# Attention on one Trainium2 core: the products with v of two key tiles at a time behind every second step

## What is computed

```python
q = h @ wq / sqrt(d); k = h @ wk; v = h @ wv        # 16 heads of 32
q, k = rotary_pos_emb(q), rotary_pos_emb(k)
logits = einsum('bhik,bhjk->bhij', q, k)
a = softmax(logits, axis=-1)
y = einsum('bhij,bhjv->bhiv', a, v)
```

## Time and profile before

| what | value |
|---|---|
| median of three runs | 3582.47 us (3579.41 to 3586.3) |
| the profiled execution's own time | 3573.79 us |
| its span | 3572.0 us |
| granted TensorE clock over the span | 0.979 of full speed |
| attention in the span | about 387 to 2061 us |
| TensorE (PE) busy | 3420.8 us, 96% |
| VectorE (DVE) busy | 2079.4 us, 58% |
| ScalarE (ACT) busy | 1508.5 us, 42% |
| GpSimd (POOL) busy | 2016.5 us, 56% |

### The profile page before, as it was taken

The page is one execution under the profiler, slowest core; times in us unless marked ns, Lnnn a source line. Parts: engine busy times, 40 slices in busy tenths (PEclk is TensorE's granted clock), DMA queues, the critical chain, the costliest instruction groups (busy, mean ns, idle before and its releaser), DMA issues. The chain is left out here.

```text
span 3572.0 us, 47047 instructions
## 1 busy us (share of the span) xinstructions
PE 3420.8 (96%) x16632; PEld 2230.6 (62%) x16632; DVE 2079.4 (58%) x3331; ACT 1508.5 (42%) x2785; POOL 2016.5 (56%) x1613
## 2 busy tenths in 40 slices
PE   6999899999999999999999959999999995999998
PEld 5777455454554555545455348888888883778877
DVE  6776677777777777777777344222222213454554
ACT  2332466666666666666666632111111112222221
POOL 3644488887978888797888812222222223343342
PEclk9999999999999999999999979999999997999999
DMA  5556677869678686867865543122222114222221
GB/s 193 177 169 205 118 154 138 148 129 154 140 131 152 127 156 133 151 142 132 156 127 107 113 140 107 55 73 75 73 67 75 54 36 139 83 86 76 73 87 41
DMA packets 176737, 419.32 MB, mean 117 GB/s; under 512 B 15382, under 2 KB 62998, under 8 KB 151670
## 3 DMA queue, kind: packets, MB, share of 16 engines
q1 hardware_dynamic: 153606, 249.59, 26.4%
q0 software_dynamic: 22896, 166.73, 24.0%
HBM read 162.25 MB, written 87.03 MB: 70 GB/s over the span
## 5 line engine op out<-in xcount | busy, mean ns | idle before, releaser
L868 DVE TENSOR_REDUCE part_max<-ps_att 128x1 f32<-128x512 f32 x1972 | 1225.4, 683 | 372.2 <-PE ps_att L786 372.1
L914 ACT ACTIVATE probs<-ps_att 128x512 f32<-128x512 f32 x2048 | 1061.7, 603 | 521.9 <-PE ps_att L758 458.7
L965 POOL TENSOR_TENSOR prob_sums<-prob_sums,probs 128x512 f32<-128x512 f32 x884 | 1142.8, 1537 | 60.8 <-DMA probs<-probs 60.8
L810 PE MATMUL ps_att<-probs,v_tok 128*32 128x512 f32 x4096 | 548.3, 607 | 3.1 <-DMA v_tok<-v 3.1
L1456 POOL TENSOR_TENSOR ff_g_lo<-ff_g,ff_g_hi 128x512 fp32r<-128x512 f32 x128 | 164.7, 1287 | 551.5 <-DVE ff_g_hi L1417 551.5
L758 PE MATMUL ps_att<-q_stack,k_stack 97*128 97x512 f32 x768 | 319.8, 424 | 9.9 <-ACT probs L914 9.7
L758 PE MATMUL ps_att<-q_stack,k_first 97*128 97x512 f32 x768 | 324.7, 423 | 2.6 <-ACT probs L914 2.6
L1325 ACT ACTIVATE ff_g<-ps_ff 128x512 f32<-128x512 f32 x128 | 76.5, 597 | 582.2 <-PE ps_ff L1209 582.2
L786 PE MATMUL ps_att<-k_stack,q_stack 96*128 96x512 f32 x768 | 303.8, 396 | 0.0
L786 PE MATMUL ps_att<-k_first,q_stack 96*128 96x512 f32 x756 | 301.9, 399 | 0.0
L1946 POOL TENSOR_TENSOR av_gated_lo<-av_full,av_gated_hi 128x512 fp32r<-128x512 f32 x64 | 94.4, 1475 | 313.9 <-ACT av_gated_hi L1783 313.9
(11 more groups left out here) (209 smaller groups left out, 5514.9 us busy)
## 6 DMA issues: line engine op xcount, KB each, us to landing
probs<-probs POOLq DMA_DIRECT2D x159, 1024.0 KB, 8.6
q_stack<-qk SPq DMA_DIRECT2D x144, 128.0 KB, 6.9
qk<-rot_hi SPq DMA_DIRECT2D x64, 256.0 KB, 7.0
qk<-rot_lo SPq DMA_DIRECT2D x64, 256.0 KB, 5.0
av_gate_rows<-gate SPq DMA_DIRECT2D x64, 256.0 KB
k_stack<-qk SPq DMA_DIRECT2D x24, 512.0 KB, 10.4
k_first<-qk SPq DMA_DIRECT2D x18, 512.0 KB, 10.1
x_in_sb<-in_x SPq DMA_DIRECT2D x8, 1024.0 KB, 6.7
```

The source lines that it names most:

```text
L810: mm = nc.tensor.matmul(o_ps[rows, :], t["v"][:, steps[w]["b"], k, rows], t["p"][:, w % PR, h, :], start=(k == 0), stop=(k == LT - 1))
L868: nc.vector.tensor_reduce(t["pm"][:, r, k:k + 1], mx[mx_uses % 3], AX.X, ALU.max)\
L914: nc.scalar.activation(t["p"][:, at % PR, h, :], sT[(at * G + h) % 3], ACT.Exp)\
L965: nc.gpsimd.tensor_tensor(x, first, t["p"][:, w % PR, h, :], ALU.add).then_inc(s["acc_done"], 1)
```

## The change

In the loop over the steps on TensorE the products with v are no longer made in each step for the step before. They are made at every second step (even `at`), for the two steps before, behind that step's scores and maxima. The sums of TensorE move with them. The two products whose place in the loop depends on other conditions, `last_sums` (at step 5 of a block) and `turn_maxima` (at step 13), stay where they are. At the end of the loop the last two tiles are done in one go. No other engine's instructions change, and their number and operands stay the same.

```diff
@@ -839,20 +839,21 @@
                     score(st, at, i)
                     if st["job"]:
                         maxima(st, i)
-                if at:
-                    values(at - 1)
-                    if by_pe(at - 1):
-                        sums(at - 1)
-                    if at >= LT and at % LT == LAST_AT:
-                        last_sums(at // LT - 1)
+                for w in (at - 2, at - 1) if at and at % 2 == 0 else ():
+                    values(w)
+                    if by_pe(w):
+                        sums(w)
+                if at >= LT and at % LT == LAST_AT:
+                    last_sums(at // LT - 1)
                 if ending is not None:
                     turn_maxima(ending)
                     ending = None
...
-            values(end - 1)
-            sums(end - 1)
+            for w in (end - 2, end - 1):
+                values(w)
+                sums(w)
             last_sums(blocks - 1)
```

## The result

| | before | changed |
|---|---|---|
| median | 3581.69 us (5 runs) | 3604.6 us (5 runs) |
| ratio | | 1.0069, 95% interval 1.0056 to 1.0083 |
| profiled execution, own time | 3573.79 us | 3602.55 us |
| its span | 3572.0 us | 3600.7 us |

A forecast was written before the change was run, and what follows sets the result against it. TensorE's own instruction list was taken to bound the kernel; terms of 11 + 15 + 0 + 1 - 3 + 8 = +32 us on 3582.5 gave 3614 us, with an 8-in-10 range of 3586 to 3640.

The forecast's parts named there:

- What TensorE alone would save: Ordinary pair of attention steps: 5.83 instead of 6.14 us by TensorE's own times, a saving of 0.31 per pair.
- Term A: Ordinary pairs: maxima loads wait for VectorE's reductions on three banks, pair 6.20 instead of 6.14; +11 us (-9 to +22).
- The rule on loads pulled ahead: Maxima weight loads: if pulled ahead even past a semaphore, a pair would be at 6.09 and Term A at -9.
- Term B: Pair with the turn, steps 13 and 14: turn and copy inside the run, pair 6.62, +0.48 each; +15 us (+2 to +22).
- Term C: Pair of steps 5 and 6: last_sums leaves the run four and four as before; 0.
- Term D: Last 19 steps, without maxima: scores wait for exponentials, pair 5.52 against 5.38; +1 us (0 to +2).
- Term E: Start: step 2's scores run while the first v product waits 3.06 us for v's load; -3 us (0 to -6).
- Term F: GpSimd's chain starts 2.3 us later; some 1.3 reaches ScalarE in seven units that load; +8 us (0 to +16).
- Rival 1: Ordinary pairs: maxima waits do not bind and the saving arrives, 3521 us, or 3570 with half; chance 0.08 together.
- Rival 4: Last stretch: TensorE's clock drops through short idles; 25 steps taking twice 3.07 add 77 us, 3691 us; chance 0.02.

The follow-up runs named there:

- The two combined versions without spread loads: Changed kernel with maxima ahead of scores, turn in step 12, last sums at step 6: 3569.07 us; also with tile 0's v product in step 1: 3565.0 us.
- The combined version with spread loads: Changed kernel with maxima first, turn in step 12, last sums at step 6, tile 0's v product in step 1, loads spread over 54 steps: 3555.66 us.

## Why the prediction was right

The sum said +32 us with a range of +4 to +58; it is +23 between the medians. The mechanism that carried 26 of the 32, VectorE's pace against three banks, is the one found, and the two runs with shorter reductions and the run with the turn moved show it. The terms for the start, the end and GpSimd came out otherwise one by one. That their sum fits, +6 forecast (D, E and F) and 3 + 1.6 + 2 in the split of the profiles above, is luck.

- **What TensorE alone would save** (0.31 a pair): right. With the reductions out of the way a pair took 5.79 against 5.83.
- **Term A** (+11): right in mechanism and size. 6.19 for 6.20, the loads released 0.06 after the reduction. Against 6.14 it is 0.05 a pair, 9 us.
- **The rule on loads pulled ahead**, from the Trainium skill, "TensorE: Matmul & The Clock Gate", in its part on what happens when a matmul is issued: in the rows shown no load passed its semaphore; the load unit (PEld) stood idle 0.28 to 0.30 ahead of each of the last three maxima loads of a run. A load that waits is not pulled ahead here.
- **Term B** (+15): right as the sum of the pair, 6.60 for 6.62, 0.46 x 31 = 14. The run with the turn in step 12 took 0.33 of it back.
- **Term C** (0): right. In the trace the pair with the last sums takes 7.01 (1212.54 to 1219.55); before, two steps and the sums took 6.99 (1195.70 to 1202.69).
- **Term D** (+1): too small; the last two blocks cost 3.0. The pair is 5.50 as worked out (5.52). What was missed is the clock, 1.7 of the 3.0: see the last section.
- **Term E** (-3): right in kind, too small. The idle before the first v group fell from 3.06 to 1.66 and the products behind it ran at full clock (granted clock 1.00 from 396 to 404 us, against 0.66 and 0.50 in its halves before). With spread loads the first block gained 4.0 net (60.68 to 56.65), -4.8 without its 0.8. In the changed kernel itself that was more than eaten within the same block (+1.6 without its 0.8), where ScalarE waited 3.69 us for GpSimd and then three times 0.63 or 0.64:

```profile
420.12 0.60 ACT L915 ACTIVATE probs<-ps_att 128x512 f32<-128x512 f32 x1 [3.69 <-POOL prob_sums L966]
```

- **Term F** (+8): the step that came out least as told: "some 1.3 of it reach ScalarE, in seven units that load". The chain does start later, GpSimd waited 167 us for v instead of 129, but its waits for the pairs' DMAs fell from 126 to 113 us, and ScalarE's waits for GpSimd from 62.6 to 28.1. What it costs stands in one place, the first block of the attention: the wait just shown. All six kernels profiled with tile 0's product at step 2 and the loads in their old place have it, 3.69 to 5.17 us long; the two with tile 0 early, those with the loads spread and those without the change have none above 1.1 there. Tile 0 early makes that block 3.3 and 4.5 us shorter (60.53 against 63.82, 58.82 against 63.35). In the later blocks that load nothing of the kind is shown: late blocks come to 17.7 us against 15.5 and 26 in two profiles without the change, and with the loads spread the distance of the two kernels did not shrink. Over the whole run the net price is about 0, within some 6 us. Between the two profiled executions the change costs 28.8 us of the forecast 32. The medians say 23, against a kernel before that is mostly slower than the execution profiled; what those slower ones lose is shown by no trace, but 24 us of the kernel before's time and 21.5 of the changed one's go with the spread of the loads.
- **Rival 1** (the saving arrives) was the right way to ask: it hung on one point, VectorE's 0.60 against 0.47, and the shorter reduction moved exactly that.
- **Rival 4** (the clock): wrong as a cause of the main loss, but present on a small scale at the end, where it takes 1.7 us here and some 5 or more in three of the versions: see the last section.

## What to carry to other kernels

Grouping work on the busiest engine to save its changes of kind takes from the other engines the pauses in which they caught up: a partner that needs 0.60 per product kept up with bursts of four on three banks, and did not with bursts of eight, though it was busy only 1244 of the attention's 1674 us. Whether a fourth bank would have done as much as a shorter reduction was not run. So cost a burst by the partner's pace and the depth of the ring between them, from the first product to the last, and move what shares the ring (here the turn) out of the burst. And look at transfers that run beside a transfer on the path, on another queue too: the profile's page has 166.73 MB on queue 0, which the 159 pairs' DMAs of 1 MB fill, and the loads on queue 1, and still spreading the loads took 24 us off the kernel before, more than any new order on TensorE tried here with the loads where they were.

## What was not expected of the hardware

In the last stretch, without maxima, the granted clock fell once for some microseconds, in a v group with sums behind it. In the changed kernel the row from 2079 to 2085 us has 0.72 (seventh column), with 1.00 on both sides:

```profile
2076.00:2079.00 3.00, 2.69 (x7) 0.93 (x6) 0.00 (x0) 2.91 (x7) 1.25 (x2) 1.00 0.01 3
2079.00:2085.00 6.00, 6.00 (x36) 1.65 (x35) 0.00 (x0) 1.12 (x3) 3.72 (x4) 0.72 0.01 3
2085.00:2090.00 5.00, 4.70 (x43) 1.38 (x41) 0.00 (x0) 2.66 (x5) 0.00 (x0) 1.00 0.00 0
```

0.72 is a mean of full clock (2.4 GHz) and half (1.2 GHz). Eight v instructions and the eight sums behind them took 3.4 (2079.13 to 2082.55) where they take 1.7 elsewhere, so 1.7 us are lost. The changed kernel with spread loads has the same in the same stretch, one pair earlier: a v group of 3.43 instead of 1.92:

```profile
2054.20 3.43 PE L810 MATMUL ps_att<-probs,v_tok 128*32 128x512 f32 x16
```

TensorE had idled 0.31 us ahead of it, as in each pair there. The kernel before has idles of the same length in each step and kept 1.00 throughout.

It is no accident of one trace, and it is what sets the length of the last block. The profiles of the kernel before, plain, with half reductions and with spread loads, show no such fall in the last block. The changed kernel, the one with spread loads and the four with half reductions, the turn moved either way or tile 0 early have one each, and a last block of 48.7 to 48.8. The two combined versions without spread loads have three and 52.1 to 52.3. The version with maxima first has four, 53.69 in all:

```profile
2031.74 3.51 PE L810 MATMUL ps_att<-probs,v_tok 128*32 128x512 f32 x16
2039.13 3.23 PE L810 MATMUL ps_att<-probs,v_tok 128*32 128x512 f32 x16
2052.27 3.49 PE L810 MATMUL ps_att<-probs,v_tok 128*32 128x512 f32 x16
2065.71 3.60 PE L810 MATMUL ps_att<-probs,v_tok 128*32 128x512 f32 x16
```

The combined version with spread loads and the one with half reductions and spread loads have none, and a last block of 47.14. So each fall costs 1.6 to 1.7 us, and only kernels with the products of two tiles in a row had any in that block. Why it falls in some of their pairs and not in others is not settled.
